# Gated cross-attention and a routed feed-forward on one core: token pieces in two buffers, routing matmuls in a bank of their own, value groups in other heads

## What is computed

```python
x = x + tanh(g_xattn) * xattn(ctx, layernorm(x))
x = x + tanh(g_ffn) * ffn(layernorm(x))
...
q = ln @ Wq + bq                                   # xattn: 16 batches, 256 tokens, 8 heads of 128
k, v = split(concat([xn, ln]) @ Wkv + bkv)         # xn: 77 media rows, normalised; ln: the tokens
out = softmax(q @ k.T * DH ** -0.5) @ v @ Wo + bo
...
scores = sigmoid(x @ router_weight.T)              # ffn: 8 experts in 2 groups, 2 experts per token
routed = sum over the 2 chosen experts of weight * down(silu(gate) * up)
y = routed + shared(x)
```

## Time and profile before

| | before |
|---|---|
| median of 3 runs | 1068.31 us (1066.63 to 1073.54) |
| the profiled execution | 1067.82 us |
| its span | 1066.1 us |
| mean granted TensorE clock in it | 0.957 |

### The profile page before, as it was taken

How to read it: one execution, slowest core, us unless ns; L and a number is a source line. 1 busy time by engine, 2 the same in 40 slices (tenths; PEclk the granted TensorE clock), 3 DMA queues, 4 the chain that set the end, 5 groups by cost and what they waited for, 6 DMA issues and landing times. The chain is left out here.

```text
span 1066.1 us, 23693 instructions
## 1 busy us (share of the span) xinstructions
PE 919.6 (86%) x6288; PEld 838.9 (79%) x6288; DVE 690.9 (65%) x1846; ACT 668.2 (63%) x1699; POOL 691.6 (65%) x1045
## 2 busy tenths in 40 slices
PE   4889898988898979797979797979798986999986
PEld 4788887878787878686868686868687875898985
DVE  5656566767675757666767666666757564867675
ACT  5767676766665666666666666666767664154643
POOL 3866475757576666667575747585848575577676
PEclk9999999999998999999999899999999997999998
DMA  6567565434342434333323333333333344889693
GB/s 189 117 146 174 128 141 130 108 56 105 58 99 48 96 65 96 65 84 71 85 67 86 75 79 82 78 82 68 85 72 82 59 88 123 254 269 320 185 296 120
DMA packets 255653, 123.38 MB, mean 116 GB/s; under 512 B 213740, under 2 KB 235487, under 8 KB 255584
## 3 DMA queue, kind: packets, MB, share of 16 engines
q1 hardware_dynamic: 244864, 101.18, 40.8%
q0 software_dynamic: 8064, 21.25, 5.4%
q10 hardware_dynamic: 2656, 0.14, 0.2%
HBM read 39.87 MB, written 33.63 MB: 69 GB/s over the span
## 5 line engine op out<-in xcount | busy, mean ns | idle before, releaser
L495 POOL TENSOR_TENSOR pn<-prob,rinv 128x333 f32<-128x333 f32 x256 | 185.5, 749 | 261.3 <-DVE rinv L1058 260.7
L502 POOL TENSOR_TENSOR pl<-pn,ph 128x333 f16<-128x333 f32 x256 | 202.2, 812 | 0.0
L651 ACT ACTIVATE ph<-prob,rinv 128x333 f16<-128x333 f32 x256 | 133.0, 568 | 30.2 <-DVE rinv L1058 27.4
L856 DVE SCALAR_TENSOR_TENSOR v_lo<-ps_g,vscale,v_hi 128x512 f16<-128x512 f32 (+1 forms) x96 | 71.9, 749 | 119.8 <-ACT v_hi L643 119.6
L657 ACT ACTIVATE prob<-ps_s,nmax 128x333 f32<-128x333 f32 x128 | 69.0, 539 | 108.3 <-DVE nmax L862 108.2
L1221 PE MATMUL ps_k<-ln_hi,w_hi 128*128 128x334 f32 x256 | 88.0, 344 | 41.6 <-POOL ln_lo L444 38.6
L842 DVE SCALAR_TENSOR_TENSOR k_lo<-ps_k,vecs,k_hi 128x334 fp32r<-128x334 f32 x128 | 72.2, 564 | 65.2 <-ACT k_hi L628 63.7
L1221 PE MATMUL ps_ar<-pth,v_hi 128*128 128x256 f16 (+1 forms) x384 | 106.9, 278 | 1.2 <-DVE o_lo L1022 1.2
L628 ACT ACTIVATE k_hi<-ps_k,vecs 128x334 fp32r<-128x334 f32 x128 | 69.2, 541 | 58.8 <-PE ps_k L1221 58.1
L1221 PE MATMUL ps_ar<-pth,v_lo 128*128 128x256 f16 (+1 forms) x384 | 105.1, 274 | 0.0
L1221 PE MATMUL ps_ar<-ptl,v_hi 128*128 128x256 f16 (+1 forms) x384 | 104.9, 273 | 0.0
(11 more groups left out here) (387 smaller groups left out, 3234.2 us busy)
## 6 DMA issues: line engine op xcount, KB each, us to landing
xin<-by_first SPq DMA_DIRECT2D x32, 130.0 KB, 3.3
xin<-by_second SPq DMA_DIRECT2D x14, 260.0 KB, 4.0
x_all<-in_x_dram SPq DMA_DIRECT2D x7, 512.0 KB, 3.9
rows_turned<-x2t_hi SPq DMA_DIRECT2D x13, 256.0 KB, 2.4
rows_turned<-x2t_lo SPq DMA_DIRECT2D x13, 256.0 KB, 2.4
w_hi<-rows_turned SPq DMA_DIRECT2D x13, 256.0 KB, 3.1
w_lo<-rows_turned SPq DMA_DIRECT2D x13, 256.0 KB, 3.6
x_all<-by_first SPq DMA_DIRECT2D x12, 260.0 KB
```

The costliest lines, as they stand in the source:

```text
L495: pool.tensor_tensor(pn[:, i, 0:KEYS], prob[:, h % 2, i, 0:KEYS], rinv[:, h % 2, i:i + 1].to_broadcast([P, KEYS]), ALU.mult).then_inc(norm ...
L502: pool.tensor_tensor(pl[:, h % 2, i, 0:KEYS], pn[:, i, 0:KEYS], ph[:, h % 2, i, 0:KEYS], ALU.subtract).then_inc(pl_ready, 1)
L651: act.activation(ph[:, par, i, 0:KEYS], prob[:, par, i, 0:KEYS], ACT.Identity, scale=rinv[:, par, i:i + 1]).then_inc(ph_ready, 1)
L856: dve.scalar_tensor_tensor(out=v_lo[0:rows, half, j, :], in0=ps_v[0:rows, :], scalar=vscale[0:rows, 0:1], in1=v_hi[0:rows, half, j, :], op ...
```

## The change

- `ln_hi` and `ln_lo` get a second buffer; batch b uses buffer b % 2, handed down as `q`. The loop takes two batches per turn, so that the buffer is known when the code is written.
- The preparation of the next batch moves forward: statistics in head 6 and aggregation in head 7 of the batch before, deviations in head 0, `z` in heads 1 and 2, the two turnings in heads 3 and 4, `ln_hi` and `ln_lo` in head 5. Batch 0 has a table of its own (`FIRST`), one head later.
- Value groups: 0 and 1 of the next batch in heads 6 and 7, 2 to 5 of the batch in heads 0, 2, 3 and 5. Heads 1 and 4 have none. Group 0 waits for the low halves (`lnlo_ready`).
- The turnings, `turn2`, `route2` and `count2` use `ps_x`, the second bank of `ps_ar`. The row sums that lay there move behind the scores in the bank of `ps_s0`, in one buffer instead of two. The waits of the routing matmuls for the second exponential, and the scores' waits for the routing, go.
- The remaining x tiles are asked for two at a time in heads 0 to 3 of batch 0, and the media rows one or two heads earlier.

```diff
-VG_AT = {7: 0, 0: 1, 1: 2, 2: 3, 3: 4, 4: 5}
+FIRST = dict(recip=1, z0=2, z12=3, turn0=4, turn1=5, hi=6, lo=6, media=4)
+LATER = dict(recip=0, z0=1, z12=2, turn0=3, turn1=4, hi=5, lo=5, media=3)
+VG_FIRST = {0: 1, 1: 2, 2: 3, 3: 4, 5: 5}
+VG_LATER = {0: 2, 2: 3, 3: 4, 5: 5}
...
+def _when(b):
+
+    return FIRST if isinstance(b, int) and b == 0 else LATER
+
+
+def _value_group(b, h):
+
+    early = isinstance(b, int)
+    if h >= 6:
+        g = h - 7 if early and b == 0 else h - 6
+        return (b + 1, g) if g >= 0 and _live(b + 1, BATCH) else None
+    at = VG_FIRST if early and b < 2 else VG_LATER
+    return (b, at[h]) if h in at and _live(b, BATCH) else None
...
-        ln_hi = sb("ln_hi", [P, FC, KPAD], F32R)
-        ln_lo = sb("ln_lo", [P, FC, KPAD], F32R)
+        ln_hi = sb("ln_hi", [P, 2, FC, KPAD], F32R)
+        ln_lo = sb("ln_lo", [P, 2, FC, KPAD], F32R)
...
+        rsum, rraw = ps_s[0][:, KPAD:KPAD + TT], ps_s[0][:, KPAD + TT:KPAD + 2 * TT]
...
-        ps_av = ps_ar[:, 0, :]
-        rsum = ps_ar[:, 1, 0:2 * TT].rearrange("p (q i) -> p q i", q=2)
-        rraw = ps_ar[:, 1, 2 * TT:4 * TT].rearrange("p (q i) -> p q i", q=2)
+        ps_av, ps_x = ps_ar[:, 0, :], ps_ar[:, 1, :]
...
-                if h == 6 and _live(b + 1, BATCH):
-                    tokens_lo(b + 1)
+                if h == _when(b)["lo"] and _live(b + 1, BATCH):
+                    tokens_lo(b + 1, 1 - q)
...
-            with pool.Fori(LOOP0, ROUTED + 1) as b:
-                for h in range(HEADS):
-                    step(b, h)
+            with pool.Fori(LOOP0, ROUTED, 2) as b:
+                for q in range(2):
+                    for h in range(HEADS):
+                        step(b + q, h, q)
...
-                _wait(act, qk_projected, 2 * HEADS * b)
-                _wait(act, v_projected, VGROUPS * b)
-                act.activation(ln_hi[:, :, :], lnf[:, :, :], ACT.Copy).then_inc(lnhi_ready, 1)
+                _wait(act, qk_projected, 2 * HEADS * (b - 1))
+                _wait(act, v_projected, VGROUPS * (b - 1))
+                act.activation(ln_hi[:, q, :, :], lnf[:, :, :], ACT.Copy).then_inc(lnhi_ready, 1)
...
-                if h == 0 and _live(b + 1, BATCH):
+                if h == 0 and isinstance(b, int) and b == 0:
                     statistics(b + 1)
+                if h == 6 and _live(b + 2, BATCH):
+                    statistics(b + 2)
...
-            def project_v(b, g):
+            def project_v(b, g, q):
                 half, j = divmod(g, 3)
                 if g == 0:
-                    pe.wait_ge(tok_scaled, 2 * FC * (b + 1))
+                    pe.wait_ge(lnlo_ready, FC * (b + 1))
+                if isinstance(b, int) and b == 0 and g == 0:
+                    pe.wait_ge(tok_scaled, 2 * FC)
                 else:
                     pe.wait_ge(vlo_ready, VGROUPS * b + g)
...
-            def route2(b, s):
+            def route2(b):
...
                 pe.wait_ge(x2lo_ready, b - 1)
-                pe.wait_ge(exp_ready, 2 * s + 2)
```

More of the change, by code:

```diff
@@ L341, in _ @@
                         keep_turned(b)
-                    if h == 5 and _live(b + 2, BATCH):
+                    if b == 0 and 2 * h < REST:
+                        for n in range(2 * h, min(2 * h + 2, REST)):
+                            rest_of_x(n)
+                    if h == _when(b)["media"] and _live(b + 2, BATCH):
                         next_media(b)
-                    if b == 0 and h < REST:
-                        rest_of_x(h)
                     if b == 1:
@@ L688, in step @@
                     turned2(b)
[L689 to L693, removed]
+                if _value_group(b, h):
+                    v_piece(*_value_group(b, h))
+                for c in range(FC):
+                    if h == _when(b)["turn%d" % c] and _live(b + 1, BATCH):
+                        turned_tokens(b + 1, c)
                 if h == 6 and _live(b - 1, ROUTED):
@@ L773, in _ @@
                 for h in range(HEADS):
-                    step(b, h)
-            with act.Fori(LOOP0, ROUTED + 1) as b:
-                for h in range(HEADS):
-                    step(b, h)
+                    step(b, h, b % 2)
+            with act.Fori(LOOP0, ROUTED, 2) as b:
+                for q in range(2):
+                    for h in range(HEADS):
+                        step(b + q, h, q)
             def split_ffn_hi(n):
@@ L1190, in _ @@
                 for h in range(HEADS):
-                    step(b, h)
+                    step(b, h, b % 2)
                     if b == 1 and h == 0:
                         consts_made()
-            with dve.Fori(LOOP0, ROUTED + 1) as b:
-                for h in range(HEADS):
-                    step(b, h)
+            with dve.Fori(LOOP0, ROUTED, 2) as b:
+                for q in range(2):
+                    for h in range(HEADS):
+                        step(b + q, h, q)
             for b in range(ROUTED + 1, BATCH):
                 for h in range(HEADS):
-                    step(b, h)
+                    step(b, h, b % 2)
             for h in range(3):
-                step(BATCH, h)
+                step(BATCH, h, 0)
                 if h == 0:
@@ L1343, in step @@
                 if _live(s + 1, STEPS):
-                    project_qk(s + 1, (h + 1) % HEADS, b + 1 if h == HEADS - 1 else b)
+                    project_qk(s + 1, (h + 1) % HEADS, b + 1 if h == HEADS - 1 else b, 1 - q if h == HEADS - 1 else q)
                 if h == 7 and _live(b - 1, ROUTED):
-                    turn2(b, s)
+                    turn2(b)
                 if h == 0 and _live(b - 2, ROUTED):
-                    route2(b, s)
+                    route2(b)
                 if h == 1 and _live(b - 3, ROUTED):
-                    count2(b, s)
-                bv = b + 1 if h == 7 else b
+                    count2(b)
                 if isinstance(b, int) and b == 0 and h == 2:
                     pe.wait_ge(wlo_pool, 2)
-                if h in VG_AT and _live(bv, BATCH):
-                    project_v(bv, VG_AT[h])
-                if h == 5 and _live(b + 1, BATCH):
-                    turn_tokens(b + 1, 0)
+                if _value_group(b, h):
+                    project_v(*_value_group(b, h), 1 - q if h >= 6 else q)
+                for c in range(FC):
+                    if h == _when(b)["turn%d" % c] and _live(b + 1, BATCH):
+                        turn_tokens(b + 1, c)
                 last = isinstance(s, int) and s - 2 == STEPS - 1
@@ L1395, in _ @@
             pe.wait_ge(wlo_pool, 1)
[L1396 removed]
+            project_v(0, 0, 0)
             for h in range(HEADS):
[L1398 removed]
+                step(0, h, 0)
             for b in range(1, LOOP0):
                 for h in range(HEADS):
[L1401 to L1404 removed]
+                    step(b, h, b % 2)
+            with pe.Fori(LOOP0, ROUTED, 2) as b:
+                for q in range(2):
+                    for h in range(HEADS):
+                        step(b + q, h, q)
             for b in range(ROUTED + 1, BATCH):
                 for h in range(HEADS):
[L1407 removed]
+                    step(b, h, b % 2)
             first_gate_up(0)
             for h in range(3):
[L1410 removed]
+                step(BATCH, h, 0)
             first_gate_up(1)
```

146 lines of the change are left out of this document (67 added, 79 removed).

## The result

The changed kernel takes 1029.45 us (median of 4 runs, 1027.95 to 1031.0) against 1068.65 for the kernel before, timed together with it: ratio 0.963, 95% interval 0.959 to 0.966. The forecast was 1022.6, so the change saved 39 of the 45 us that were forecast. The profiled execution has a span of 1027.5 us.

A forecast was written before the change was run, and what follows sets the result against it. GpSimd's serial stretch of 19.14 us from head 3 to the row copy was taken as the bound. Savings of 1.0 + 2.9 + 4.6 + 34.2 + 2.5 = 45.2 from 1067.8 gave 1022.6 us, range 982 to 1047.

The forecast's parts named there:

- Low halves in head 5, and the wait that takes the place: TensorE's value group in head 6 finds GpSimd's pieces 24.5 us after head 3's start, idling 5.7; part 4.3 us dearer.
- The clock after the wait: After head 6's wait TensorE's clock is at 0.50 for 3.45 us, losing 1.72 us, as after the earlier 2.67 idle.
- Heads 0 to 2: These heads of a steady batch fall from 19.50 to 16.94 us, without routing waits and head 1's value group.
- The routing term: Routing and counting matmuls in heads 0 and 1 no longer wait for the second exponential: 0.58 us each saved.
- Turning in its own bank: Turnings in heads 3 and 4: TensorE's 1.43 us stall goes, but by itself brings nothing after batch 2.
- Batches 0, 1, 2 and 15: Batches outside the steady ones were to save 1.0, 2.9, 4.6 and 2.5 us.
- Edits at nothing: Moved statistics, small sums, x tiles in twos and the loop of two batches: costed at nothing, each within 1 us per batch.
- Contention: GpSimd's low-probability products beside VectorE's subtraction take 0.25 us more, 12 x 0.25 = 3 us, kept for the range.
- Rival 1: TensorE's clock does not fall after head 6's wait: 20.6 us less, 1002; chance 0.15.
- Rival 2: GpSimd's stretch is not the bound and TensorE runs full: a batch takes 44.8 us, total 931; chance 0.08.
- Rival 3: GpSimd's stretch grows and eats the gain: 1035 with contention, 1068 at 3.8 us per batch; chance 0.07.
- Rival 4: Clock stays low to the end of head 7 after the longer idle: 88 us on top, 1110; chance 0.06.

The follow-up runs named there:

- run 1: Changed kernel with GpSimd's low-half piece of head 5 ahead of the masking and the row copy: 1008.87 us, ratio 0.942.
- run 2: Changed kernel with a second copy of the rows into a spare tile on GpSimd: 1044.1 us, ratio 0.976.
- run 3: Changed kernel with 24 extra matmuls, results unused, before the value group's wait in 12 batches: 1004.57 us, ratio 0.940.
- run 12: Run 4 without the loop: 1043.97 us, ratio 0.976.
- run 7: Changed kernel with both turnings, low halves and first value group a head later in all batches, as in batch 0: 1054.93 us, ratio 0.987.
- run 11: Changed kernel with batches 4 to 13 written out, no loop: 1020.28 us, ratio 0.953.
- run 4: Changed kernel with routing and counting matmuls waiting for the second exponential again, still in their own bank: 1060.69 us, ratio 0.994.
- run 9: Run 6 with head 6's comparison also behind the query half on VectorE: 951.69 us, ratio 0.889.
- run 10: Run 9 with GpSimd's bias addition in head 7 and batches 4 to 13 written out: 926.35 us, ratio 0.865.
- run 6: Changed kernel with both low-half pieces on VectorE and the shift behind the query half of head 6: 981.6 us, ratio 0.919.

## Why the prediction was right, and where it was off

**What bounds the kernel.** This part is shown: TensorE's stalls in head 5 were beside GpSimd's stretch, and runs 1 and 2 move the time with the stretch. GpSimd was 67% busy and still set the pace.

**Low halves in head 5, and the wait that takes the place.** TensorE was to find the pieces 24.5 us after head 3's start and to idle 5.7. It restarts after 469.89 - 445.06 = 24.83 (24.58 in batch 9) and idles 5.5.

**The clock after the wait: the step that was mis-sized.** "I take the same loss here", 1.72, was carried over from one shorter wait before. The loss is 1.8 in batch 8, 3.0 in batch 9, and 2.2 in the mean by run 3. The prediction had named a clock that is low for much more than 3.5 us as a sign of being wrong, and this sign is there: it was low for 6.8, of which 3.6 to 6.1 lie beside work in batches 3 to 14. So head 7 starts after 29.57 and 30.38 where 29.2 was forecast, and the part is 4.6 to 5.5 us dearer than before, not 4.3. Of the 5.5 us that batches 3 to 14 fell short, (1.8 + 3.0) / 2 - 1.72 = 0.7 per batch or 8 us come from here (6 by run 3's mean); heads 0 to 2 gave some 2 back.

**Head 7** takes 6.08 and 6.22 (forecast 6.06). **Heads 0 to 2** take 497.46 - 480.71 = 16.75 (16.94). The routing term was too small: put back by themselves, the waits cost 0.72 and 0.74 (run 12).

**Turning in its own bank.** "By themselves they bring nothing after batch 2": run 7 agrees, the stall comes back at head 7.

**Batches 0, 1, 2 and 15** came within 0.3 us each. The 0.7 us before batch 0 can't be put down to the change: that start lies between 21.3 and 23.2 us in the runs that share it.

**Edits at nothing.** For the loop of two this was too low. VectorE does stand at its turn; the routing matmuls no longer wait for the exponential, so TensorE does not stand there with it. But run 11 shows that the loop costs the changed kernel 9.2 us by another way: GpSimd's stretch starts later in head 3 and the value group with it. Part of this the loop of one had too (4.36 us into head 3 before, 4.35 to 4.59 now, 4.20 without a loop); how much it cost there was not run. Runs 4 and 9 show the price of the turn itself once nothing covers it, about 2 us and more.

**Contention.** GpSimd's piece took 1.00 in place of 0.89, some 12 x 0.11 = 1.3 us of the 3 that were kept for it. The low-probability products, for which they were kept, took 1.54 to 1.56 in batch 8's stretch, as without contention.

**The rivals.** Rival 1 (the clock does not fall) is what run 3 brings about, 1004.6 against its 1002. Rival 2 (TensorE full) is what run 10 brings about with its further edits, 926 against its 931. Rival 3 did not come: the stretch has its 19.13 us. Rival 4 did not either: the low clock ends before head 7's scores or within 0.3 us of their start.

## What to carry to other kernels

A wait that is removed from one engine moves to the next operation that needs the same late producer; so look for the producer's serial stretch, not for the wait, and take out of the stretch, or from behind it, every operation for which the bounding engine queues. Before an operation that waits is moved, list what else on its engine waits for the same stretch: here two more stood behind the first, and moving only one gained nothing. And an idle of several microseconds on TensorE costs more than its length, as the granted clock comes back late.

## What the runs showed of the hardware

**The low clock varies after equal waits.** After idles of 5.5 us the clock fell 2.3 us into the wait in batch 8 and 4.8 in batch 9, and was low for 6.8 both times; with idles of 4.3 (run 1) it was low for 3.4 or 6.8, with 6.0 to 6.6 (run 2) for 6.8 or 10.2. The price of one wait is therefore a range.

**A turn of a loop of two batches is not free.** VectorE behind the turn into batch 8 and at the change to batch 9 inside the body, in the changed kernel:

```profile
431.15 0.51 DVE L880 TENSOR_REDUCE nmax<-ps_s 128x1 f32<-128x333 f32 x1 [2.35 <-issue]
...
481.54 0.51 DVE L880 TENSOR_REDUCE nmax<-ps_s 128x1 f32<-128x333 f32 x1 [0.26 <-PE ps_s L1246]
```

In the kernel before, whose loop holds one batch, VectorE has no such idle at its turns. At the turn into batch 8:

```profile
449.11 0.50 DVE L862 TENSOR_REDUCE nmax<-ps_s 128x1 f32<-128x333 f32 x1 [0.71 <-PE ps_s L1221]
```

The instruction queue q14 moved 39 packets before and 83 after. The trace places them: five move between 426.9 and 432.6 us, around the turn shown, and one of these between 430.5 and 431.1, just before VectorE goes on at 431.15; from 270 to 780 us it moves 48 in the changed kernel and 2 in the kernel before. So VectorE seems to wait for instructions that are fetched again at the turn. This is a coincidence in time: run 11, which takes the loop away and the idle with it, does not part the two.

**VectorE stands behind a GpSimd instruction.** In the changed kernel the shift of two columns starts with GpSimd's row copy (467.75, 1.03):

```profile
467.75 1.05 DVE L901 SCALAR_TENSOR_TENSOR shift<-mv,rstd 128x2 f32 x1 [3.46 <-POOL rstd L436]
```

In run 11 it starts before the copy (at 466.39, the copy at 466.52) and takes 0.18, and there the comparison behind it takes 1.05 beside the copy, where the changed kernel's takes 0.28:

```profile
466.39 0.18 DVE L899 SCALAR_TENSOR_TENSOR shift<-mv,rstd 128x2 f32<-128x2 f32 x1 [3.24 <-POOL rstd L436]
466.65 1.05 DVE L949 TENSOR_TENSOR cmp<-choice 128x128 f32<-128x128 f32 x1
```

So VectorE was held for the whole of GpSimd's instruction. The Trainium skill (SBUF — State Buffer, "Who interferes with whom") says that of a VectorE instruction with two SBUF inputs and a GpSimd instruction that reads SBUF the later one stands still until the other ends; the trace agrees here with its 1.05 beside 1.03. The smaller price that the prediction took, 0.25, was read from GpSimd's side alone; VectorE's subtraction took 1.04 there, and its two in run 6 took 0.49 and 0.55. The hold-up cost the changed kernel nothing that the rows show: VectorE's key half for head 7 ends at 469.48, before TensorE restarts at 469.89.
